# Normalising attention weights on VectorE before the transposes, in a four-layer Trainium2 kernel

## The chip, the cores and the metric

The kernel runs on one NeuronCore of one Trainium2 chip, as one program. The time is the device time of one execution in microseconds (us), the median of three runs. Engines: TensorE (PE, its weight loads are PEld), VectorE (DVE), ScalarE (ACT), GpSimd (POOL), and the DMA queues, most of them issued from SyncE (SP).

## What is computed

Sixteen sequences of 128 tokens with 512 features go through four residual updates: gated cross attention with 16 heads of 32 over a 128-token context, a ternary feed-forward layer, an attention over features, and a mixture of 16 experts. The change lies in the first, which the kernel interleaves with the second:

```python
q = (x @ wq.T).reshape(B, L, NH, HD)
k = (memory_tokens @ wk.T).reshape(B, M, NH, HD)
v = (memory_tokens @ wv.T).reshape(B, M, NH, HD)
attn = jnp.einsum('blhd,bmhd->bhlm', q, k) * scale
attn = jnp.where(memory_mask[:, None, None, :], attn, -jnp.inf)
attn = jax.nn.softmax(attn, axis=-1)
out = jnp.einsum('bhlm,bmhd->blhd', attn, v).reshape(B, L, C)
out = out @ wo.T
gate = jax.nn.sigmoid(x @ wg.T)
return gate * out
```

The ternary layer normalises each row of x, rounds it to 8 bits, and multiplies by weights of -1, 0 and 1. All projections of the attention are computed in three matmuls each (high by high, high by low, low by high part of each operand), so every operand is split by ScalarE (high part) and VectorE (the rest).

## The kernel before

`attention_heads_and_ternary` holds the first two layers. One list of steps, `plan`, is written out by hand as text, once for a group of four batches (GB = 4) and four times over (NG = 4, groups 0 to 3). Every engine walks the same list in the same order and does its own part of each step, so a step's place in the text is its place in the queue of every engine that has work in it. An engine stands still at a wait, and everything behind it in its queue stands still too. A number after a step is a batch, a half batch or a quarter batch (a unit of four heads), counted in the group; negative numbers are batches of the group before. `during` adds steps that only group 0 has: statistics of x (`sx`), scales (`xa`, `xb`, `xd`) and the ternary weights (`fq`, `ft`, `fg`).

The steps that matter here, with their work:

- `xT.b`, `cT.b`: four transposes on PE into a bank T, a ScalarE copy (high part), a VectorE subtraction (low part, L701).
- `q.p.j`, `k.p.j`: 12 matmuls on PE into a bank M, then a ScalarE copy (L591). `g.b`, `v.b`, `oP.b`: 12 wider matmuls into a bank M, emptied by ScalarE (`g`, L585) or VectorE (`v` L730, `oP` L737). `fm`: four bf16 matmuls, emptied by VectorE (L744).
- `Sa.t`, `Sb.t`: the score matmuls of a half batch. The step between the two, always a transpose, gives the first half time to drain. They fill both score banks SC.
- `sm.u`: for a unit of four heads VectorE takes the maxima (L753) and subtracts them (L758) into `pr`, ScalarE takes four exponentials in place and lets their sums accumulate (L597).
- `pT.u`: four transposes of `pr` into T, a ScalarE copy into `pT` (L569). `pv.t`: 8 products of attention weights and values, issued as 16 matmuls, into `O` (L530).
- `rc.b`: VectorE takes the reciprocals of the 16 sums of a batch (L763). `bc.b`: PE spreads them over a bank `REC`, in the layout of `O`, by 16 products with the identity, issued as 32 matmuls (L539); ScalarE copies the bank to `o` (L602). `on.b`: VectorE multiplies `O` by `o` (L767). `oT.b`: ScalarE rounds `o` to the high part (L606), VectorE subtracts (L771). `oP.b` multiplies by Wo.
- `u.b`: the quantising of a batch, six VectorE instructions that wait for each other (L652 to L659); `uT.b` transposes it. `ra`, `rb`, `rd`: row scales, seven, three and one small VectorE instruction with a GpSimd power between them. `st`, `sf`, `sx`: row statistics (L708). `nm`: normalised x. `mk`: mask rows.
- GpSimd adds `upd` to X after every `oP` and `fm` (L386, L394) and a bias in `uT` (L390). SyncE loads the next pair of contexts at each odd `cT` and the next masks at each fourth `mk`.

There are two banks T, two M, two SC, one O and one REC, eight in all. A step of kind T or M takes the bank of the step but one before it in the order of T or M steps, and waits until that one has been emptied, for `xT` and `cT` by both ScalarE and VectorE:

```python
tf = at(T_KINDS, s)
wait(pe, t_hi, tf - 2)
wait(pe, t_lo, up_to(T_KINDS, SPLIT, tf - 2))
```

Of the kernel before, what the change touches and what calls it, by code (L numbers as in the profile page):

```python
# [140 lines left out]
def attention_heads_and_ternary(nc, c, x, g_x, g_f, fw, fb, ctx_in, mask, norm_w, wq, wk, wv, wo, wg):  # L141

    X, identF = c["X"], c["identF"]
    with ExitStack() as st:
# [159 lines left out]
        with nc.Block() as block:  # L304
# [92 lines left out]
            def _(pe):  # L397
# [55 lines left out]
                for s in plan:  # L453
# [3 lines left out]
                    elif kind in T_KINDS:  # L457
# [63 lines left out]
                    elif kind == "pv":  # L521
                        b, half = t // 2, t % 2
                        pe.wait_ge(t_hi, at(T_KINDS, ("pT", 2 * t + 1)))
                        if half == 0:
# [7 lines left out]
                        i.then_inc(pv, 1)
                    elif kind == "bc":
                        pe.wait_ge(o_norm, 2 * t + 1)
                        wait(pe, r_out, t)
                        for j in range(KC):
                            for r in range(HQ):
                                at_ = col_of(j, r)
                                i = pe.matmul(REC[r * HD:(r + 1) * HD, j * S:(j + 1) * S],  # L539
                                              rec[:, t % 2, at_:at_ + 1].to_broadcast([P, HD]), identF[:, :],  # L540
                                              start=True, stop=True)
# [1311 lines left out]
```

## Time and profile before

| | us |
|---|---|
| median of 3 runs | 1397.67 |
| lowest and highest run | 1394.35 and 1404.95 |
| time of the profiled execution | 1401.04 |
| its span in the profile | 1399.3 |
| group 0 of the heads, from its first `Sa` to the next group's | 107.80 |
| group 1 | 103.25 |
| group 2 | 101.81 |
| group 3, first half and second half | 45.58 and 50.32 |

The profile is one execution. The profiled execution's own time lies 1.7 us above its span, and 3.4 us above the median of the runs. The four groups take from 40.4 to 449.2 us of the span. After them follow the last steps of the ternary layer, the attention over features, and the experts, which take more than half of the span.

### The profile page before, as it was taken

What the parts mean: (1) busy time and instruction counts of PE and PEld (TensorE: products, weight loads), DVE (VectorE), ACT (ScalarE), POOL (GpSimd) and SP (SyncE); (2) the same over time, 40 slices, a digit from 0 to 9 for tenths busy, and PEclk for the clock granted to TensorE, in tenths of its full rate; (3) what the DMA queues carried; (4) which work ended last, traced back from release to release, by engine and by line L of the source; (5) the groups of instructions that cost most, each with busy time, mean ns of one, the idle gap of its engine ahead of it and who ended that gap; (6) DMA issues with size and microseconds to landing.
All of it is one profiled execution on the core that took longest, in us unless ns stands there. A gap on an engine that the chain in (4) does not pass through costs nothing. (4 is left out here: it accounts for less than half of the span.)

```text
span 1399.3 us, 25475 instructions
## 1 busy us (share of the span) xinstructions
PE 1238.7 (89%) x7821; PEld 1041.0 (74%) x7822; DVE 719.3 (51%) x1443; ACT 553.9 (40%) x1430; POOL 426.3 (30%) x504
## 2 busy tenths in 40 slices
PE   6998999999996599789987896799999989999992
PEld 6876777777774377556766675689999878999992
DVE  5666655655655599854667532433234543434330
ACT  4543444444542388632111011433334543434340
POOL 1101211211212556520035601134444433344442
PEclk9999999999998699889999998899999999999996
DMA  9000000000000111322000202455446655545456
GB/s 319 24 22 12 17 1 18 17 1 17 1 2 1 46 42 41 115 88 73 1 0 1 92 30 77 143 140 137 76 80 139 182 124 143 137 82 131 88 137 165
DMA packets 53881, 103.62 MB, mean 74 GB/s; under 512 B 5127, under 2 KB 20999, under 8 KB 53751
## 3 DMA queue, kind: packets, MB, share of 16 engines
q1 hardware_dynamic: 38182, 65.78, 14.2%
q0 software_dynamic: 15632, 36.97, 13.9%
q8 instruction: 40, 0.66, 0.2%
q14 instruction: 27, 0.21, 0.0%
HBM read 75.99 MB, written 30.93 MB: 76 GB/s over the span
## 5 line engine op out<-in xcount | busy, mean ns | idle before, releaser
L1703 PE MATMUL t_H<-m_W,t_xT 128*128 128x352 f32 x1632 | 286.6, 332 | 15.8 <-DVE m_W L1781 14.1
L1703 PEld LDWEIGHTS t_H<-m_W,t_xT 128*128 128x128 f32 x1632 | 268.2, 193 | 18.1 <-DVE m_W L1781 14.6
L1670 POOL DMA_INDIRECT acc_d<-t_ys,t_sid x68 | 109.4, 1609 | 284.6 <-ACT t_ys L1732 200.7
L1748 ACT ACTIVATE t_sl<-t_H 128x352 f32<-128x352 f32 x68 | 31.5, 464 | 174.6 <-PE t_H L1703 174.6
L597 ACT ACTIVATE pr<-pr 128x128 f32<-128x128 f32 x256 | 76.1, 299 | 55.3 <-DVE pr L758 53.9
L62 PE MATMUL t_Y<-m_W,t_hT 128*128 128x512 f32 (+1 forms) x207 | 88.6, 428 | 9.9 <-DVE t_hT L1826 6.8
L1802 DVE TENSOR_TENSOR t_h<-t_H,t_sl 128x352 f32<-128x352 f32 x68 | 35.6, 523 | 106.3 <-ACT t_sl L1748 105.7
L1732 ACT ACTIVATE t_ys<-t_Y,t_wcol 128x512 f32<-128x512 f32 x69 | 47.4, 687 | 95.5 <-PE t_Y L64 88.1
L1824 DVE TENSOR_TENSOR t_hT<-t_TH,t_hT 128x256 fp32r<-128x256 f32 x68 | 28.8, 423 | 106.5 <-ACT t_hT L1769 105.3
L64 PE MATMUL t_Y<-m_W,t_hT 128*128 128x512 f32 (+1 forms) x207 | 82.6, 399 | 0.0
L63 PE MATMUL t_Y<-m_W,t_hT 128*128 128x512 f32 (+1 forms) x207 | 82.3, 398 | 0.0
L1644 POOL DMA_INDIRECT t_xg<-rows_d,t_gid x72 | 71.2, 990 | 22.1 <-issue 21.8
L386 POOL TENSOR_TENSOR X<-X,upd 128x512 f32<-128x512 f32 x16 | 20.4, 1273 | 157.0 <-DVE upd L737 157.0
L1161 POOL TENSOR_SCALAR m_W<-m_W,bst 128x128 fp32r<-128x128 f32 x64 | 55.7, 889 | 29.7 <-PE eL L1225 29.6
L373 POOL TENSOR_TENSOR tmp<-tmp,nhalf 128x2 f32<-128x2 f32 (+2 forms) x22 | 18.6, 848 | 144.9 <-DVE tmp L627 121.1
L753 DVE TENSOR_REDUCE mx<-SC 128x4 f32<-128x512 f32 x64 | 43.7, 684 | 32.7 <-PE SC L517 32.6
L569 ACT ACTIVATE pT<-T 128x512 f32<-128x512 f32 x64 | 38.0, 595 | 54.4 <-PE T L423 54.2
L1556 DVE SCALAR_TENSOR_TENSOR X<-eY,tg,X 128x512 f32<-128x512 f32 x32 | 23.9, 751 | 63.5 <-PE eY L64 63.4
L1280 ACT ACTIVATE ehT<-eh 128x512 fp32r<-128x512 f32 (+1 forms) x24 | 15.2, 633 | 99.8 <-DVE eh L1498 99.8
L1777 DVE TENSOR_TENSOR t_xT<-t_TX,t_xT 128x512 fp32r<-128x512 f32 x69 | 47.6, 690 | 12.1 <-issue 7.3
L62 PEld LDWEIGHTS t_Y<-m_W,t_hT 128*128 128x128 f32 (+1 forms) x207 | 39.6, 191 | 16.9 <-DVE m_W L1818 7.5
L1725 ACT ACTIVATE t_xT<-t_TX 128x512 fp32r<-128x512 f32 x69 | 41.4, 599 | 24.5 <-PE t_TX L1682 24.5
...
## 6 DMA issues: line engine op xcount, KB each, us to landing
...
m_r<-in_L_ffn_w_dram SPq DMA_DIRECT2D x13, 512.0 KB, 6.8
...
CT<-in_ctx_dram SPq DMA_DIRECT2D x8, 512.0 KB, 3.7
...
```

Source lines behind the costliest of these rows:

```text
L62: pe.matmul(out, lhs(0), rhs(0), start=first, stop=False)
L63: pe.matmul(out, lhs(0), rhs(1), start=False, stop=False)
L64: return pe.matmul(out, lhs(1), rhs(0), start=False, stop=last)
L597: i = act.activation(pp, pp, ACT.Exp, scale=SCALE0, accum_out=sums[:, t // HQ % 2, at_:at_ + 1])
L753: dve.tensor_reduce(mx[:, t % 2, :], bk, AX.X, ALU.max).then_inc(s_out, 1)
L1161: i = pool.tensor_scalar(tab_a[t % SLOTS][:, k, :], iP.bitcast(F32), place_p[:, t, k:k + 1], None, ALU.is_equal)
L1644: pool.indirect_dma_start(out=xg[:, b, :], out_offset=None, in_=m["rows_d"][:, :], in_offset=bass.IndirectOffsetOnAxis(ap=gid[:, b:b + 1], ...
L1670: pool.indirect_dma_start(out=m["acc_d"][:, :], out_offset=bass.IndirectOffsetOnAxis(ap=sid[:, b:b + 1], axis=0), in_=ys[:, b, :], in_offs ...
L1703: x_ = pe.matmul(bk[b % 2][:, 0:I], xT[:, b % 2, jx, k, :], W13[:, jw, k, j, :], start=k == 0 and jx == jw, stop=k == KC - 1 and jx == 1)
L1725: act.activation(xT[:, b % 2, 0, :, :], TX[:, :].rearrange("p (k t) -> p k t", k=KC), ACT.Copy).then_inc(tx_hi, 1)
L1732: act.activation(ys[:, (b - 1) % UT, :], Y[(b - 1) % 2][:, :], ACT.Copy, scale=wcol[:, (b - 1) % UT:(b - 1) % UT + 1]).then_inc(y_evac, 1)
L1777: dve.tensor_tensor(xT[:, b % 2, 1, :, :], TX[:, :].rearrange("p (k t) -> p k t", k=KC), xT[:, b % 2, 0, :, :].bitcast(F32), ALU.subtract) ...
```

## The change

The attention weights are divided by their sums before they are transposed. A new step `nr.u`, one for each unit of four heads (16 in a group), has VectorE take the four reciprocals of the unit and, after a wait for them, multiply the 128x512 tile `pr` in place by the reciprocals, broadcast along the keys. `pT.u` waits for this (`p_norm`) instead of the exponentials. `rc`, `bc` and `on` are gone, with the tile `o` and the bank REC. O gets that bank as its second one, alternating by batch, and `oT` reads O directly, on ScalarE and VectorE. `pv` of a batch waits for the `oT` of the batch two before. The text of the plan is written anew: `oP.2` and `g.3` move, most odd `pT` stay between `Sa` and `Sb`, most even ones move to just before `Sa`, `cT.3` moves ahead of `pT.0`, `fq.1` behind `v.1`.

```diff
         for g in range(NG):
             d = during.get(g, ("",) * 10)
             plan += steps(
-                f"Sa.0 xT.2 Sb.0 sm.0 sm.1 v.0 st.-2 st.-1 cT.2 ra.-1 xT.3 {d[0]} g.0 rb.-1 pT.0 cT.3 q.1.0 rd.-1 Sa.1 pT.1 Sb.1 "
-                f"sm.2 sm.3 mk.4 q.1.1 u.-2 {d[1]} pv.0 q.1.2 sf.-4 sf.-3 pT.2 uT.-2 u.-1 {d[2]} q.1.3 Sa.2 pT.3 rc.0 Sb.2 sm.4 sm.5 "
-                f"fm.-2 bc.0 pv.1 on.0 oT.0 k.1.0 uT.-1 {d[3]} k.1.1 pT.4 {d[4]} v.1 fm.-1 Sa.3 pT.5 Sb.3 sm.6 sm.7 mk.5 "
-                f"k.1.2 nm.4 nm.5 pv.2 k.1.3 pT.6 sf.-2 {d[5]} g.1 oP.0 Sa.4 pT.7 rc.1 Sb.4 sm.8 sm.9 "
-                f"xT.4 sf.-1 v.2 bc.1 pv.3 on.1 oT.1 pT.8 {d[6]} cT.4 g.2 xT.5 Sa.5 pT.9 Sb.5 sm.10 sm.11 mk.6 "
-                f"oP.1 cT.5 st.0 pv.4 q.2.0 pT.10 {d[7]} q.2.1 Sa.6 pT.11 rc.2 Sb.6 sm.12 sm.13 "
-                f"q.2.2 nm.6 nm.7 bc.2 pv.5 on.2 oT.2 {d[8]} q.2.3 st.1 pT.12 v.3 {d[9]} ra.0 Sa.7 pT.13 Sb.7 sm.14 sm.15 mk.7 "
-                f"k.2.0 rb.0 pv.6 k.2.1 rd.0 u.0 pT.14 uT.0 u.1 g.3 pT.15 rc.3 oP.2 bc.3 pv.7 on.3 oT.3 fm.0 k.2.2 uT.1 k.2.3 fm.1 "
-                f"oP.3 ", g)
+                f"Sa.0 xT.2 Sb.0 sm.0 sm.1 v.0 st.-2 st.-1 nr.0 cT.2 nr.1 ra.-1 xT.3 {d[0]} g.0 rb.-1 cT.3 pT.0 rd.-1 "
+                f"Sa.1 pT.1 Sb.1 sm.2 sm.3 mk.4 q.1.0 sf.-4 sf.-3 q.1.1 nr.2 u.-2 {d[1]} nr.3 q.1.2 pv.0 uT.-2 u.-1 {d[2]} q.1.3 pT.2 "
+                f"Sa.2 pT.3 Sb.2 sm.4 sm.5 fm.-2 oT.0 k.1.0 nr.4 uT.-1 {d[3]} pv.1 k.1.1 nr.5 v.1 {d[4]} fm.-1 pT.4 "
+                f"Sa.3 pT.5 Sb.3 sm.6 sm.7 mk.5 k.1.2 nm.4 nr.6 nm.5 pv.2 k.1.3 nr.7 sf.-2 {d[5]} g.1 oP.0 pT.6 "
+                f"Sa.4 pT.7 Sb.4 sm.8 sm.9 xT.4 sf.-1 v.2 nr.8 oT.1 pv.3 nr.9 {d[6]} cT.4 g.2 xT.5 pT.8 "
+                f"Sa.5 pT.9 Sb.5 sm.10 sm.11 mk.6 oP.1 cT.5 nr.10 st.0 pv.4 q.2.0 nr.11 {d[7]} q.2.1 pT.10 "
+                f"Sa.6 pT.11 Sb.6 sm.12 sm.13 q.2.2 nm.6 nr.12 nm.7 pv.5 q.2.3 oT.2 nr.13 {d[8]} st.1 g.3 v.3 {d[9]} ra.0 pT.12 "
+                f"Sa.7 pT.13 Sb.7 sm.14 sm.15 mk.7 k.2.0 rb.0 pv.6 k.2.1 nr.14 rd.0 u.0 oP.2 nr.15 uT.0 u.1 k.2.2 pT.14 fm.0 uT.1 "
+                f"pT.15 k.2.3 pv.7 fm.1 oT.3 oP.3 ", g)
...
@@ tensor
                         elif kind == "pT":
-                            pe.wait_ge(p_exp, t + 1)
+                            pe.wait_ge(p_norm, t + 1)
...
                         if half == 0:
                             pe.wait_ge(m_dve, at(BY_DVE, ("v", b)))
-                            wait(pe, o_norm, 2 * b)
+                            wait(pe, o_lo, b - 1)
...
@@ scalar
-                            pp, at_ = pr[:, t % 2, slot, :], t % HQ * HQ + slot
-                            i = act.activation(pp, pp, ACT.Exp, scale=SCALE0, accum_out=sums[:, t // HQ % 2, at_:at_ + 1])
+                            pp = pr[:, t % 2, slot, :]
+                            i = act.activation(pp, pp, ACT.Exp, scale=SCALE0, accum_out=sums[:, t % 2, slot:slot + 1])
...
                     elif kind == "oT":
-                        act.wait_ge(o_norm, 2 * t + 2)
+                        act.wait_ge(pv, 2 * t + 2)
                         wait(act, m_fill, at(M_KINDS, ("oP", t - 1)))
-                        act.activation(oT[:, 0, :, :].rearrange("p k t -> p (k t)"), o[:, :], ACT.Copy).then_inc(o_hi, 1)
+                        act.activation(oT[:, 0, :, :].rearrange("p k t -> p (k t)"), O[t % 2][:, :], ACT.Copy).then_inc(o_hi, 1)
...
@@ vector
+                    elif kind == "nr":
+                        dve.wait_ge(p_exp, t + 1)
+                        pp = pr[:, t % 2, :, :]
+                        dve.reciprocal(rec[:, t % 2, :], sums[:, t % 2, :]).then_inc(inverse, 1)
+                        dve.wait_ge(inverse, t + 1)
+                        dve.tensor_tensor(pp, pp, rec[:, t % 2, :].unsqueeze(2).to_broadcast([P, HQ, S]), ALU.mult)\
+                            .then_inc(p_norm, 1)
```

## Rows read from the trace of the kernel before

**Rows 1.** The page, part 1: engine, busy us, share, instructions.
```profile
PE 1238.7 (89%) x7821; PEld 1041.0 (74%) x7822; DVE 719.3 (51%) x1443; ACT 553.9 (40%) x1430; POOL 426.3 (30%) x504
```

**Rows 2.** Windows, groups 0, 1, 3: PE, PEld, DVE, ACT, POOL busy, clock, DMA.
```profile
40.44:148.24 107.80, 98.14 (x872) 80.85 (x873) 69.61 (x160) 49.55 (x190) 17.21 (x14) 0.98 0.06 19
148.24:251.49 103.25, 98.33 (x865) 79.92 (x865) 59.66 (x126) 47.55 (x184) 18.05 (x16) 0.98 0.04 12
353.30:398.88 45.58, 43.91 (x369) 35.51 (x369) 26.91 (x56) 21.95 (x89) 7.76 (x7) 1.00 0.00 1
398.88:449.20 50.32, 42.20 (x385) 31.84 (x384) 27.61 (x58) 21.06 (x83) 9.24 (x9) 0.90 0.01 1
```

**Rows 3.** Timeline: start us, duration us, engine, line, operation; from 241.5 us.
```profile
241.53 1.08 PE L539 MATMUL REC<-identF,rec 128*32 128x128 f32 x32
242.43 0.62 PE L530 MATMUL O<-pT,va 128*32 128x128 f32 x16
```

**Rows 4.** VectorE by line, 148 to 252 us: count, busy, mean ns, idle before.
```profile
L771 DVE TENSOR_TENSOR oT<-o,oT 128x512 fp32r<-128x512 f32 x4 | 2.8, 693 | 2.8 <-ACT oT L606 2.8
L767 DVE TENSOR_TENSOR o<-O,o 128x512 f32<-128x512 f32 x4 | 2.8, 690 | 3.6 <-ACT o L602 3.6
L763 DVE RECIPROCAL rec<-sums 128x16 f32<-128x16 f32 x4 | 1.0, 244 | 0.0
```

**Rows 5.** Timeline of VectorE, 162 and 166 us.
```profile
162.03 0.69 DVE L753 TENSOR_REDUCE mx<-SC 128x4 f32<-128x512 f32 x1 [2.01 <-PE SC L517]
162.76 0.69 DVE L758 TENSOR_TENSOR pr<-SC,mx 128x512 f32<-128x512 f32 x1
163.36 0.68 DVE L753 TENSOR_REDUCE mx<-SC 128x4 f32<-128x512 f32 x1
...
166.49 0.16 DVE L658 RECIPROCAL fsc<-fsc 128x1 f32<-128x1 f32 x1
166.69 0.48 DVE L659 TENSOR_SCALAR fu<-fu,fsc 128x512 f32<-128x512 f32 x1
```

**Rows 6.** Timeline, how a transpose waits for its bank, 156.8 us.
```profile
156.80 0.60 PE L423 MATMUL T<-identF,pr 128*128 128x128 f32 x4
157.10 0.69 DVE L701 TENSOR_TENSOR xT<-T,xT 128x512 fp32r<-128x512 f32 x1
157.89 0.63 PE L423 MATMUL T<-identF,CT 128*128 128x128 f32 x4 [0.50 <-issue]
```

**Rows 7.** Timeline, how a projection waits for ScalarE, 182.9 us.
```profile
182.93 0.71 PE L517 MATMUL SC<-kT,qT 32*128 32x128 f32 x8
...
185.20 0.64 PE L530 MATMUL O<-pT,va 128*32 128x128 f32 x16
...
188.06 0.19 PEld L62 LDWEIGHTS M<-Wg,xT 128*128 128x128 f32 x1 [0.38 <-ACT kT L591]
...
190.94 0.40 PE L62 MATMUL M<-Wo,oT 128*128 128x512 f32 x1
```

**Rows 8.** Timeline, a transpose waiting for VectorE at 233.6 us.
```profile
233.59 1.08 PE L423 MATMUL T<-identF,fu 128*128 128x128 f32 x4 [2.78 <-DVE fu L659]
```

**Rows 9.** Window behind that wait: busy by engine, then granted clock.
```profile
234.00:236.00 2.00, 2.00 (x8) 1.71 (x7) 1.23 (x2) 0.60 (x1) 0.00 (x0) 0.50 0.00 0
```

**Rows 10.** Timeline of group 0, a reduction that starts late.
```profile
108.19 0.71 PE L517 MATMUL SC<-kT,qT 32*128 32x128 f32 x8
...
111.87 0.63 DVE L753 TENSOR_REDUCE mx<-SC 128x4 f32<-128x512 f32 x1
```

**Rows 11.** L845 beside busy GpSimd: duration ns min/median/max; one slow instance.
```profile
L845 DVE TENSOR_TENSOR as<-asg,as x66: 673/678/1068, 480.8 to 580.1; 128x512 fp32r<-128x512 f32 x66
...
483.44 1.07 DVE L845 TENSOR_TENSOR as<-asg,as 128x512 fp32r<-128x512 f32 x1 [0.67 <-ACT as L901]
...
484.14 1.51 POOL L875 TENSOR_TENSOR ak<-aCX,ak 128x512 fp32r<-128x512 f32 x1 [0.18 <-POOL ak L873]
```

**Rows 12.** The page, part 6: a context load, KB and us to landing.
```profile
CT<-in_ctx_dram SPq DMA_DIRECT2D x8, 512.0 KB, 3.7
```

More of the change, by code:

```diff
@@ L170, in attention_heads_and_ternary @@
         mx = sb("mx", [P, 2, HQ])
-        sums, rec = sb("sums", [P, 2, NH]), sb("rec", [P, 2, NH])
-        o = sb("o", [P, D])
+        sums, rec = sb("sums", [P, 2, HQ]), sb("rec", [P, 2, HQ])
         oT = sb("oT", [P, 2, KC, S], F32R)
@@ L185, in attention_heads_and_ternary @@
         T, M, SC = bank("T", 2), bank("M", 2), bank("SC", 2)
-        O, REC = bank("O", 1)[0], bank("REC", 1)[0]
+        O = bank("O", 2)
         mask_f = dg[0:NB, :]
@@ L201, in attention_heads_and_ternary @@
         NU, NH2 = NB * HQ, 2 * NB
-        TILED = ("xT", "cT", "v", "g", "rc", "bc", "on", "oT", "oP", "st", "sf", "sx", "nm", "mk", "u", "uT", "fm")
+        TILED = ("xT", "cT", "v", "g", "oT", "oP", "st", "sf", "sx", "nm", "mk", "u", "uT", "fm")
         def steps(text, g):
@@ L221, in steps @@
                         continue
-                elif kind in ("sm", "pT"):
+                elif kind in ("sm", "nr", "pT"):
                     nums[0] += NQ * g
@@ L259, in attention_heads_and_ternary @@
         M_KINDS, X_UPD, STATS = BY_ACT + BY_DVE, ("oP", "fm"), ("sx", "st", "sf")
-        PV = ("pv", "bc")
         order = {}
@@ L264, in attention_heads_and_ternary @@
             order[kinds] = {s: i + 1 for i, s in enumerate([s for s in plan if s[0] in kinds])}
-        for kinds in (SPLIT, T_KINDS, BY_ACT, BY_DVE, M_KINDS, X_UPD, STATS, PV):
+        for kinds in (SPLIT, T_KINDS, BY_ACT, BY_DVE, M_KINDS, X_UPD, STATS):
             order[kinds] = {s: i + 1 for i, s in enumerate([s for s in plan if s[0] in kinds])}
@@ L290, in attention_heads_and_ternary @@
         s_half, s_fill, s_out, p_exp, pv = (sem(n) for n in ("s_half", "s_fill", "s_out", "p_exp", "pv"))
-        o_norm, r_out, o_hi, o_lo = (sem(n) for n in ("o_norm", "r_out", "o_hi", "o_lo"))
+        inverse, p_norm, o_hi, o_lo = (sem(n) for n in ("inverse", "p_norm", "o_hi", "o_lo"))
         added, biased, q_step, f_step = (sem(n) for n in ("added", "biased", "q_step", "f_step"))
         U_STEPS, F_STEPS = 6, 8
-        RING = SC + [O, REC]
-        def col_of(j, r):
-            return (j // 2 * 2 + r % 2) * HQ + r // 2 * 2 + j % 2
+        RING = SC + O
         def ctx_after(eng, s):
@@ L529, in _ @@
                             for r in range(HQ):
-                                i = pe.matmul(O[r * HD:(r + 1) * HD, j * S:(j + 1) * S], va[:, j * HQ + r, :],
+                                i = pe.matmul(O[b % 2][r * HD:(r + 1) * HD, j * S:(j + 1) * S], va[:, j * HQ + r, :],
                                               pT[:, r % 2, r // 2 * 2 + jj, :], start=True, stop=True)
[L532 to L541, printed above, removed]
                         i.then_inc(pv, 1)
@@ L567, in _ @@
                         elif kind == "pT":
-                            wait(act, pv, at(PV, ("pv", t // 2 - 1)))
+                            wait(act, pv, at(("pv",), ("pv", t // 2 - 1)))
                             act.activation(pT[:, t % 2, :, :].rearrange("p j m -> p (j m)"), src, ACT.Copy).then_inc(t_hi, 1)
@@ L728, in _ @@
                         dve.wait_ge(m_fill, mf)
-                        wait(dve, pv, at(PV, ("pv", 2 * t - 1)))
+                        wait(dve, pv, at(("pv",), ("pv", 2 * t - 1)))
                         dve.tensor_scalar(va[:, :, :], M[(mf - 1) % 2][:, :].rearrange("p (h d) -> p h d", h=NH),
@@ L759, in _ @@
                                           ALU.subtract).then_inc(s_out, 1)
-                    elif kind == "rc":
-                        dve.wait_ge(p_exp, HQ * t + HQ)
-                        wait(dve, pv, at(PV, ("bc", t - 2)))
-                        dve.reciprocal(rec[:, t % 2, :], sums[:, t % 2, :]).then_inc(o_norm, 1)
-                    elif kind == "on":
-                        dve.wait_ge(pv, at(PV, ("pv", 2 * t + 1)))
-                        dve.wait_ge(r_out, t + 1)
-                        dve.tensor_tensor(o[:, :], O[:, :], o[:, :], ALU.mult).then_inc(o_norm, 1)
+                    elif kind == "nr":
[5 more added lines that the diff above has]
+                            .then_inc(p_norm, 1)
                     elif kind == "oT":
@@ L770, in _ @@
                         dve.wait_ge(o_hi, t + 1)
-                        dve.tensor_tensor(lo_, o[:, :], hi_.bitcast(F32), ALU.subtract).then_inc(o_lo, 1)
+                        dve.tensor_tensor(lo_, O[t % 2][:, :], hi_.bitcast(F32), ALU.subtract).then_inc(o_lo, 1)
 def attention_features(nc, c, ctx_in):
```

4 lines of the change are left out of this document (removed).

## The prediction

> **What bounds the kernel now.** I read the page first: PE is busy 89% of the span [rows 1]. Then the windows of the four groups, which hold all that the change touches: they take 408.8 us, PE is busy in 98.33 of group 1's 103.25 us and VectorE in 59.66 [rows 2]. So PE sets the pace there, and what leaves PE's queue is time won, unless PE then waits for another engine. Last I read the timeline of group 1 for the places where PE does wait. They are of three kinds.
>
> A transpose waits until its bank T is emptied. cT.3 could follow pT.0 at 157.3 but starts at 157.89, right behind VectorE's subtraction for xT.3, which ran from 157.10 to 157.79 [rows 6].
>
> A projection waits until its bank M is emptied. Behind Sb.3 (182.93) PE has k.1.2, pv.2, k.1.3 and pT.6, and then g.1 waits for a ScalarE copy until 188.06, because that copy is queued behind the eight exponentials [rows 7]. So the first copy behind a pair of sm is through 5.1 us after Sb starts.
>
> A transpose waits for the quantising: uT.0 stands 2.78 us, for VectorE [rows 8], and in the 2 us behind it the granted clock is 0.50, the lower of the two levels (1.2 GHz) [rows 9].
>
> Summed over group 1, step by step, by which a step's length is the distance to the next start less its length elsewhere, PE loses about 8.5 us in this way: 3.0 at uT.0 and 1.0 in the slow clock behind it, 1.4 at uT.-2, 0.7 at cT.3, and eight losses of 0.2 to 0.6. That is more than the 4.9 us that the window shows as not busy, since a last matmul's modelled end covers part of a wait.
>
> **What goes.** bc occupies PE from 241.53 to the next start at 242.43, 0.90 us [rows 3], 16 times: 14.4 us, 3.6 in a group. On VectorE rc (0.24) and on (0.69) go, four of each in a group [rows 4], 3.7 us busy; the copy of REC leaves ScalarE.
>
> **What comes.** No nr is in the trace. Its multiply is a 128x512 tensor-tensor with both inputs in SBUF, as L771 is: 0.69 us [rows 4]. In the queue such an instruction takes 0.60 (162.76 to 163.36), and a reciprocal with a wait behind it 0.20 [rows 5]. So nr takes 0.81 us of the queue, 16 times: 13 us in a group. VectorE's load in group 1 rises from 59.7 to about 70 of 103 us: it stays below PE on average, but each nr pushes back everything behind it, and that has a price where PE waits for it.
>
> **Where PE waits in the new order.** I laid the new text against the durations of the trace, group 1, with time from Sa.0. A step v, g or oP takes PE 2.9 us and q or k 1.6 behind Sb (182.93 + 0.65 to 185.20), 1.5 elsewhere [rows 7], S with its transpose 2.0, a transpose 0.4, pv 0.6.
> - pT.0 now takes the bank of xT.3. Before, the subtraction for xT.3 started 8.86 us after Sa.0 [rows 2, 6]; now nr.0 and nr.1 stand ahead of it, and it ends at 8.86 + 1.62 + 0.69 = 11.2. PE is there at 9.2: 2.0 us. cT.3 and pT.1 lose 0.3 each in the same way.
> - q.1.2 needs the copy of q.1.0, which is behind the exponentials of sm.3, 5.1 us after Sb.1's start [rows 7]. PE has only 0.65 + 1.6 + 1.5 until then: 1.4 us. uT.-2 then waits 0.7 for u.-2, k.1.1 0.3.
> - g.1, g.3 and oP.2 come behind a projection, pv and a projection: 0.65 + 1.6 + 0.6 + 1.5 against 5.1, 0.8 us or, with the engine's reaction, 0.9 each.
> - pT.8 takes the bank of cT.4. From Sb.4's start the exponentials end at 4.7 and ScalarE copies xT.4 until 5.3; behind it VectorE has xT.4 0.6, sf 0.6, v 0.7, nr.8 0.8, oT.1 0.6, nr.9 0.8, cT.4 0.7: 10.1. PE has Sb, xT.4, v, pv, cT.4, g, xT.5: 8.1. It loses 2.0 us, where before it lost almost none.
> - At the end of the group, oP.2 (2.9) now stands ahead of uT.0, and covers u.0: the wait of 2.78 is gone. But uT.1 waits 1.1 (oP.2's drain, nr.15 and u.1 follow each other), and oP.3 waits 1.6, as VectorE has fm.1 and oT.3 to do after fm.1 has left PE.
>
> These come to 12.5 us. Group 1: -3.6 - 8.5 + 12.5 = **+0.4 us**; group 2 the same. Group 0 has `during` as well. Already before, its reduction behind Sb.6 starts 3.7 us after Sb's start (108.19, 111.87) where 0.75 is usual, as fq.3 and four sx are in front [rows 10]; now nr.10 and nr.11 are too, and fg.3 waits 5.2 us for the copy of q.2.2. With 1.8 at pT.1, 1.4 each at q.1.2, v.1 and fg.1, 3.4 at pT.8 and the end of the group as above its waits come to about 18 us, against about 13 read before (among them 3.0 at uT.0 and 3.5 behind the late reduction); less 3.6 for bc, it ends **1.7 us** later. In group 3 xT, cT, q.2 and k.2 are absent, and its second half has PE busy only 42.2 of 50.3 us [rows 2]: PE waits on chains. There the order pays: oP.2 fills the time of u.0, g.3 that of the exponentials. The first half ends 2.2 later, as in group 1. The second goes Sa.4 to Sa.5 in 8.7 us, to Sa.6 in 6.9, to Sa.7 in 9.1 (g.3 among them), and to the end of oP.3 in 20.5: 45.2 against 50.3, and a further 1.1 because the last update no longer waits for GpSimd: 2.2 - 5.1 - 1.1 = **-4.0 us**.
>
> The steps moved past SyncE's queue are cT.3 (a step earlier) and mk; a context lands in 3.7 us [rows 12] and is used a group later, so that costs nothing. The second O bank lets pv start without `on`; PE never waited there. Nothing behind the heads changes.
>
> **GpSimd beside nr.** The trace shows that a tensor-tensor with both inputs in SBUF can be slowed: L845 takes 0.67 to 0.68 us, but 1.07 at 483.44, while GpSimd runs [rows 11]. In the new order nr.15 stands right behind oP.2's update, which sets off GpSimd's add. I take 0.4 us once a group, on the way to uT.1: **+1.6**. The lowest bound is nothing, the highest 0.4 on every nr.
> The Trainium skill ("SBUF — State Buffer", "Who interferes with whom") says that a VectorE instruction with two SBUF inputs contends with a GpSimd instruction that reads SBUF, and that the loser waits out the whole instruction. The rows agree that the two meet, but with 0.4 us, not the whole instruction. By the rule in full a meeting could cost as much as one whole GpSimd instruction, and the sum would be that of the slower rival below.
>
> **Sum.** 1.7 + 0.4 + 0.4 - 4.0 + 1.6 = +0.1 us on the profiled execution's 1401.04. The median is 3.4 us below that, 1397.67; so I predict **1398 us**, no change. The clock I take as even: the waits of 2.78 that brought 0.50 go, two of 2.0 and in group 0 one of 5 come; a 5 us wait may cost 1 to 2 us more.
>
> **The rivals.**
> - *PE keeps what it is given.* My replay may place too many waits, for it adds one late engine to another. If PE loses in the new order what it lost before, only bc counts: -14.4, 1383 us; if uT.0's 4 us go too in three groups, 1371. For it: VectorE idles 40% of the group. Against: the two subtractions at pT.0 and pT.8 are plainly behind two nr each. Chance 0.16.
> - *VectorE's lateness is the pace (slower).* Five places in a group hang on nr: pT.0 and pT.8 by two each, uT.1 by one. If nr takes c, PE loses 5 (c - 0.81) more in each. With the slow multiply throughout, c = 1.2, that is 2 us a group, 1406 us; it is slower by over 1% from c = 1.5 on: 1412. If each nr waited out a GpSimd instruction of 1.5 us [rows 11], c would be 2.3, 7.5 us a group, 1428. Against: GpSimd is busy 18 of 103 us [rows 2], so most nr meet nothing. Chance 0.13. It is the rule of the Trainium skill's page "SBUF — State Buffer" (section "Who interferes with whom") that would bring this case about.
> - *My case*, within 1%: 0.71, its own range 1388 to 1408.
>
> **How the numbers follow.** 1% is 14 us, about what a measurement of this kernel tells from no change. Faster 0.16, same 0.71, slower 0.13. A wrong reading by 2 us of each group's waits moves the time by 8; the range reaches to the edge of both rivals, 1384 to 1410.
>
> **What would show it right or wrong.** In the changed kernel: L539 gone, 64 multiplies of 0.69 us at the new line, some at 1.1 beside GpSimd; groups 1 and 2 from Sa.0 to Sa.0 in 102 to 106 us; PE standing about 2 us at pT.0 and pT.8, both released by a subtraction of L701's kind; 1.4 at q.1.2, released by ScalarE; no wait at uT.0; VectorE busy near 70 us in group 1. If the groups take 100 us or less, the replay had waits too many; if pT.8 stands 3 us or more, nr is dearer than I took it.

## The result, and the profile after

The changed kernel takes **1426.61 us** (median of 4 runs, 1425.43 to 1427.83) against 1398.74 us before on the same chip: ratio **1.0183**, 95% interval 1.0155 to 1.0211. It is 28 us slower; the prediction was 1398 us, no change. The profiled execution took 1425.57 us, its span is 1423.9.

First the page, part 1 (compare [rows 1]): PE has 512 matmul records fewer and is busy 2.6 us longer. VectorE has 46 us more.

```profile
PE 1241.3 (87%) x7309; PEld 1038.1 (73%) x7310; DVE 765.5 (54%) x1539; ACT 547.1 (38%) x1414; POOL 426.0 (30%) x504
```

The windows of the changed kernel's four groups (compare [rows 2]; the number behind the busy times is the granted clock, then DMA share and GB/s):

```profile
40.76:160.26 119.50, 103.59 (x744) 83.48 (x744) 80.14 (x184) 47.85 (x186) 17.58 (x14) 0.90 0.06 17
160.26:270.88 110.62, 100.06 (x739) 80.81 (x739) 70.96 (x150) 46.08 (x180) 18.42 (x16) 0.94 0.04 11
270.88:376.90 106.02, 94.02 (x737) 75.49 (x737) 70.94 (x150) 45.76 (x180) 18.43 (x16) 1.00 0.03 11
376.90:479.75 102.85, 89.98 (x625) 68.38 (x624) 67.31 (x138) 41.24 (x168) 18.36 (x16) 0.88 0.00 1
```

Groups 2 and 3 of the kernel before, over the same steps:

```profile
251.49:353.39 101.90, 96.99 (x866) 78.82 (x866) 59.66 (x126) 47.53 (x184) 18.05 (x16) 1.00 0.04 12
353.39:449.39 96.00, 86.21 (x753) 67.35 (x752) 54.52 (x114) 43.01 (x172) 17.19 (x16) 0.95 0.01 1
```

The four groups of these two layers, from here on called the heads, take 438.99 us instead of 408.95: **+30.0**. Groups 1 and 2 run the same plan, and VectorE, ScalarE and GpSimd are busy equally long in both; yet group 1 is 4.6 us longer and PE is *busy* 6 us longer in it, at a clock of 0.94 against 1.00. What lies outside the heads is 5.4 us shorter than before. The change doesn't touch it; behind the heads the profiled executions of kernels with the same text differ by as much (944.2 us here, 949.9 before, 946.0 and 949.8 in later ones). So below I read a cause from the heads, and the median only for the total. Each kernel has one profile, and so one reading of its heads.

The multiply of nr, and the first instruction of a quantising, by duration in ns (minimum/median/maximum), then first and last start:

```profile
L744 DVE TENSOR_TENSOR pr<-pr,rec x64: 691/692/1789, 47.0 to 463.1; 128x512 f32<-128x512 f32 x64
...
L631 DVE TENSOR_SCALAR fu<-X,mean,rstd x16: 540/546/1486, 141.2 to 490.0; 128x512 f32<-128x512 f32 x16
```

Of the 64 multiplies 56 take the 0.69 us that I took from [rows 4]. Three take 1.17 or 1.18, and five 1.76 to 1.79: one at the end of each group and one in the middle of group 3. Even L631, which the change didn't touch, goes up to 1.49.

Then the waits of PE in the changed kernel, 40 to 480 us (us in total, times, longest):

```profile
PE T L416 <- DVE fu L638: 15.7, 8, 3.2
PE T L416 <- issue: 12.4, 8, 1.8
PE M L62 <- DVE oT L749: 6.1, 4, 1.5
PE M L62 <- ACT kT L574: 4.9, 7, 1.1
PE M L430 <- ACT qT L574: 4.3, 1, 4.3
PE M L62 <- ACT qT L574: 2.6, 3, 1.4
PE T L416 <- DVE pr L744: 2.2, 1, 2.2
```

The waits are where the replay had put them: "issue" is pT.0 and pT.8 at the bank (up to 1.8), then oP.3 (1.5), g.1, g.3 and oP.2, fg.3 in group 0 (4.3, `M L430`) and q.1.2. One line is too large: eight waits for `fu` come to 15.7 us. Three of them are uT.1 in groups 0 to 2, 2.85 us each, where I had 1.1; in group 3 uT.0 and uT.1 wait 3.17 and 2.14. The timeline at the end of group 2 shows why uT.1 waits so long:

```profile
363.03 0.17 DVE L742 RECIPROCAL rec<-sums 128x4 f32<-128x4 f32 x1
363.19 1.27 POOL L379 TENSOR_TENSOR X<-X,upd 128x512 f32<-128x512 f32 x1 [4.12 <-DVE upd L716]
363.23 1.78 DVE L744 TENSOR_TENSOR pr<-pr,rec 128x512 f32<-128x512 f32 x1
...
364.42 1.71 POOL L383 TENSOR_TENSOR X<-X,fbrow 128x512 f32<-128x512 f32 x1
364.94 1.48 DVE L631 TENSOR_SCALAR fu<-X,mean,rstd 128x512 f32<-128x512 f32 x1
...
368.38 0.63 PE L416 MATMUL T<-identF,fu 128*128 128x128 f32 x4 [2.85 <-DVE fu L638]
```

GpSimd's addition for oP.2 starts 0.04 us ahead of nr.15's multiply, which takes 1.09 us more than alone. GpSimd goes straight on to the bias addition of uT.0; the first instruction of u.1 takes 1.48 instead of 0.54. Together 2.03 us on the chain to uT.1, whose transpose waits 2.85.

And the clock, in windows of the changed kernel behind such waits (groups 0 and 3):

```profile
105.50:108.50 3.00, 3.00 (x9) 2.42 (x8) 2.80 (x5) 1.43 (x9) 0.00 (x0) 0.50 0.00 0
...
125.70:128.70 3.00, 2.97 (x8) 2.49 (x9) 2.22 (x8) 1.47 (x4) 0.17 (x1) 0.50 0.00 0
...
444.50:449.00 4.50, 4.50 (x31) 3.35 (x31) 3.40 (x6) 2.45 (x14) 0.00 (x0) 0.54 0.00 0
```

0.50 is the lower level, 1.2 GHz. The first stretch follows a wait of 1.7 us at pT.8, the second one of 4.3 at fg.3, the third one of 2.2 at pT.10. PE is busy throughout, but slowly: three matmuls of a wide projection take 1.28 us from start to start there, and 0.70 elsewhere.

Such a wait is not always followed by a slow stretch. Groups 1 and 2 have the same waits at pT.0, pT.8, uT.1 and oP.3. Here is pT.0 in each:

```profile
171.46 0.63 PE L416 MATMUL T<-identF,pr 128*128 128x128 f32 x4 [1.78 <-issue]
282.07 0.63 PE L416 MATMUL T<-identF,pr 128*128 128x128 f32 x4 [1.79 <-issue]
```

Behind the first the clock falls to 0.50 until 179; behind the second, and in the whole of group 2, it stays at 1.00. What decides between the two the runs don't show.

**Theory.** Most of the 28 us is two prices that I set too low: TensorE's slow clock behind waits of 2 to 3 us, and GpSimd holding up VectorE once in a group. **Rivals.** The multiplies as such load VectorE too much; or the order of the steps is at fault, whichever mechanism it carries.

### The profile page after: what moved, and what is told of

Read it like the earlier page. It is cut to its first block and busy times, and to the rows that moved or that the text cites. A ratio compares the mean times of both kernels' runs of the same rounds, so it can differ in the third digit from the quotient of the medians.

```text
span 1423.9 us, 24472 instructions
## 1 busy us (share of the span) xinstructions
PE 1241.3 (87%) x7309; PEld 1038.1 (73%) x7310; DVE 765.5 (54%) x1539; ACT 547.1 (38%) x1414; POOL 426.0 (30%) x504
## 5 line engine op out<-in xcount | busy, mean ns | idle before, releaser
L1681 PE MATMUL t_H<-m_W,t_xT 128*128 128x352 f32 x1632 | 285.6, 331 | 15.4 <-DVE m_W L1759 13.9
L1681 PEld LDWEIGHTS t_H<-m_W,t_xT 128*128 128x128 f32 x1632 | 267.2, 192 | 17.8 <-DVE m_W L1759 14.4
L416 PE MATMUL T<-identF,pr 128*128 128x128 f32 x256 | 42.7, 292 | 14.6 <-issue 12.4
L744 DVE TENSOR_TENSOR pr<-pr,rec 128x512 f32<-128x512 f32 x64 | 51.2, 800 | 2.2
```

Of the source, the lines that this page charges most:

```text
L744: dve.tensor_tensor(pp, pp, rec[:, t % 2, :].unsqueeze(2).to_broadcast([P, HQ, S]), ALU.mult)\
L1681: x_ = pe.matmul(bk[b % 2][:, 0:I], xT[:, b % 2, jx, k, :], W13[:, jw, k, j, :], start=k == 0 and jx == jw, stop=k == KC - 1 and jx == 1)
```

## Experiments

Times are medians; the kernel before ran beside them at 1398.4 to 1399.6 us.

### e1: GpSimd's additions later

```diff
 # GpSimd, oP
                         pool.wait_ge(m_dve, at(BY_DVE, s))
+                        if t % GB == 2:
+                            pool.wait_ge(q_step, U_STEPS * (t - 1) + 1)
 # GpSimd, uT: uT.0's bias addition waits for all of u.1
-                        pool.wait_ge(q_step, U_STEPS * t + 1)
+                        pool.wait_ge(q_step, U_STEPS * (t + 2 if t % GB == 0 else t) + (0 if t % GB == 0 else 1))
```

> The changed kernel, but GpSimd holds back two adds of each group: that of oP.2 until u.1's first instruction is done, and the bias add of uT.0 until all of u.1 is done. In the changed kernel nr.15's multiply takes 1.78 us there instead of 0.69, and u.1's first instruction 1.48 instead of 0.54. Theory G (GpSimd beside VectorE's two-input multiply is what was mis-sized): both go back to 0.69 and 0.54, the wait at uT.1 falls from 2.85 to about 1 us, and four groups save 8 us, with some clock behind it up to 12: 1415 to 1419. Theory C (the clock behind long waits) alone: only what the shorter uT.1 wait saves in clock, 2 to 4 us: 1423. Theory O (the order as such): no change, 1426.

Measured: 1415.15 us, ratio 1.0112 (1.0085 to 1.0139), as the theory of the collision expected; heads 429.48, 9.5 shorter than the changed kernel's. The ten runs spread widely, from 1402.24 us at a mean clock of 0.948 to 1420.63 at 0.933, and the profile is of the slowest, so the 9.5 is a rough figure. In e1's timeline both instructions have their usual length again:

```profile
355.90 0.69 DVE L746 TENSOR_TENSOR pr<-pr,rec 128x512 f32<-128x512 f32 x1
356.51 0.54 DVE L633 TENSOR_SCALAR fu<-X,mean,rstd 128x512 f32<-128x512 f32 x1
357.08 0.69 DVE L636 TENSOR_REDUCE fsc<-fu 128x1 f32<-128x512 f32 x1
357.19 1.27 POOL L381 TENSOR_TENSOR X<-X,upd 128x512 f32<-128x512 f32 x1 [5.46 <-DVE fu L633]
```

The stretch from Sa.7 of group 2 to the next Sa.0 has the full clock in both kernels. It goes from 24.12 to 22.09 us: **2.03 us**, what the two instructions had too much in the changed kernel. The collision is shown, and its price. The last two rows also show why the addition costs nothing in its new place: beside it a reduction, with one input, takes 0.69 us, as it does alone.

### e2: filler transposes in PE's waits

```diff
+                def warm(n):
+                    b = (done_pv[0] + 1) // 2
+                    wait(pe, o_lo, b - 1)
+                    for i in range(n):
+                        pe.transpose(O[b % 2][:, i % KC * P:(i % KC + 1) * P], identF[:, :], identF[:, :])
+                WARM = {("pT", 0): 15, ("q", 1, 2): 8, ("g", 1): 3, ("pT", 8): 15, ("g", 3): 3, ("oP", 2): 4, ("uT", 1): 25,
+                        ("oP", 3): 14, ...}
 ...
                 for s in plan:
+                    if warm_of(s):
+                        warm(warm_of(s))
```

> The changed kernel, but ahead of the long waits of PE it issues transposes of the identity into the O bank that is free at that time, as many as fill the wait of the changed kernel to some tenths of a us (15 ahead of pT.0 and pT.8, 25 ahead of uT.1, 14 ahead of oP.3, 38 ahead of fg.3 in group 0). The waits themselves stay. Theory C: the granted clock stays at 1.0 in the groups, the steps behind the waits take 2.9 instead of 3.9 to 5.2 us, and the time falls by 10 to 15 us: 1411 to 1416. Theory G or O: the clock costs nothing on the path, 1426 or a little more for fillers that are too long.

Measured: 1411.13 us, ratio 1.0084 (1.006 to 1.0108). Windows of e2's groups:

```profile
40.05:152.13 112.08, 108.99 (x880) 90.73 (x881) 80.17 (x184) 47.69 (x186) 17.63 (x14) 1.00 0.07 18
152.13:258.23 106.10, 103.58 (x824) 85.01 (x824) 70.98 (x150) 45.84 (x180) 18.49 (x16) 1.00 0.04 12
258.23:364.30 106.07, 103.62 (x825) 85.02 (x825) 70.98 (x150) 45.84 (x180) 18.48 (x16) 1.00 0.04 11
364.30:462.44 98.14, 93.78 (x745) 75.15 (x744) 67.30 (x138) 41.05 (x168) 18.45 (x16) 1.00 0.00 1
```

PE has more to do and the heads are **16.6 us** shorter: 7.4, 4.5, 0.0 and 4.7 by group, just where the clock had been below 1.00. The median fell by 15.5, as the theory of the clock expected. The slow clock is shown, and its price in these executions.

### e3: the multiply left out

```diff
-                        dve.reciprocal(rec[:, t % 2, :], sums[:, t % 2, :]).then_inc(inverse, 1)
-                        dve.wait_ge(inverse, t + 1)
-                        dve.tensor_tensor(pp, pp, rec[:, t % 2, :].unsqueeze(2).to_broadcast([P, HQ, S]), ALU.mult)...
+                        dve.reciprocal(rec[:, t % 2, :], sums[:, t % 2, :]).then_inc(p_norm, 1)
```

> The changed kernel without nr's multiply: only the reciprocals are taken, and the attention weights are left undivided. VectorE has 64 instructions of 0.69 us and their 18 us of stretching less. The load theory (VectorE's added work is the loss, by whichever way): pT.0 and pT.8 wait 0.6 to 0.8 instead of 1.8, uT.1 none, at most 1398. Theory O (the new order costs by itself, at the M banks: q.1.2, g.1, g.3, oP.2): the waits at these stay, and the time stays above 1405.

The attention weights are not divided, so other tokens go to other experts and the median (1415.14) can't be read; the heads can. They take 402.65 us, with groups of 107.41, 100.44, 100.39 and 94.41, at clocks of 0.98, 1.00, 1.00 and 0.93. So with the multiply goes more than the whole loss, 36.3 us: it is the root, and the waits, the clock and the collision are the ways in which it costs. Beside e2 (group 2: 106.07) the multiply costs 5.7 us in a group at full clock. The stretch from Sa.7 has 2.0 of it, the collision; the rest lies in the stretches with pT.0 (1.5), from Sa.1 to Sa.2 (0.7) and with pT.8 (1.5). Without it the new order beats the group of before at full clock (101.90) by only 1.5 us of bc's 3.6. I put the rest down to the order's waits: in e3 the projections wait 11.7 us for ScalarE, 3.2 before, and oP.3 waits 1.5 us in each group. That is read from the lists of waits, not tested. Neither expectation asked for the heads; the waits at q.1.2 and its like stayed, as theory O had it.

### e4: nr in the order of before

```diff
-                f"Sa.0 xT.2 Sb.0 sm.0 sm.1 v.0 st.-2 st.-1 nr.0 cT.2 nr.1 ra.-1 xT.3 {d[0]} g.0 rb.-1 cT.3 pT.0 rd.-1 "
+                f"Sa.0 xT.2 Sb.0 sm.0 sm.1 v.0 st.-2 st.-1 nr.0 cT.2 nr.1 ra.-1 xT.3 {d[0]} g.0 rb.-1 pT.0 cT.3 q.1.0 rd.-1 Sa.1 pT.1 Sb.1 "
...
```

> VectorE scales as in the changed kernel, but PE's steps stand in the order of the kernel before (pT.8 ahead of cT.4, g.3 between uT.0 and pT.15, oP.2 behind pT.15, q.1.0 ahead of Sa.1), nr just ahead of where its pT needs it, nr.15 ahead of u.1 and so before oP.2's add. Theory O: without the new order the waits of PE stay at those of the kernel before plus the late subtractions, bc is saved, and the time is 1390 to 1400. The load theory: 64 nr cost wherever they stand, above 1415.

Measured: 1421.94 us, ratio 1.0165 (1.0128 to 1.0203); heads 434.78. The first waits of e4's list:

```profile
PE T L416 <- DVE pr L744: 18.7, 18, 3.5
PE T L416 <- DVE fu L638: 10.5, 6, 1.8
```

In the old order eighteen transposes wait for the multiply itself, so the even pT had a reason to move. But the new order as a whole is no better (438.99): its own waits are at the banks and the end of the group, and its clock is lower (0.90, 0.94, 1.00, 0.88 against e4's 0.94, 0.97, 0.97, 0.90). The time fits the expectation that nr costs wherever it stands; e8 below shows that it need not.

### e5: e1 and e2 together

The two edits above, with fewer fillers at uT.1 (8).

> The changed kernel with both edits at once: GpSimd's two adds held back as in e1_late_add, and the fillers of e2_fill (8 instead of 25 ahead of uT.1, since the wait there is shorter now). Two causes that add up: e2_fill's heads took 422.4 us; each group loses the 2.0 us of meeting with GpSimd at uT.1: 414 us for the heads and about 1403 in all. If GpSimd mattered in e1_late_add only through the clock (its shorter wait keeps TensorE fast, which the fillers do as well), then nothing is left to gain: 1411.

Measured: 1401.20 us, ratio 1.0017 (0.9997 to 1.0037), heads 414.13. Windows of its groups 1 and 3:

```profile
149.68:253.68 104.00, 101.63 (x807) 83.16 (x807) 68.93 (x150) 45.78 (x180) 18.07 (x16) 1.00 0.04 12
...
357.70:453.79 96.09, 92.62 (x734) 73.97 (x733) 65.25 (x138) 41.01 (x168) 18.03 (x16) 1.00 0.00 1
```

With both causes gone the time of before is back, as the first expectation had it, and group 1 takes the 103.65 us of the replay within 0.35. From e2 to e5 the heads lose 8.3 us, 2.07 a group. The two causes take 24.9 of the 30.0 us in the heads; alone they took 9.5 (e1) and 16.6 (e2), so they hardly overlap. Fillers aren't free where PE didn't wait: in group 3 nothing holds pT.8, and its 15 fillers make the stretch from Sa.4 to Sa.5 10.61 us long, 8.99 in the changed kernel.

### e6: the new order with the bank REC

```diff
 # before.py: rc, bc, on, the tile o and REC stay; the text of the plan is the changed one
+                f"Sa.2 pT.3 rc.0 Sb.2 sm.4 sm.5 fm.-2 k.1.0 uT.-1 {d[3]} bc.0 pv.1 on.0 oT.0 k.1.1 v.1 {d[4]} fm.-1 pT.4 "
...
```

> The kernel before (reciprocals spread by PE over REC, no nr) in the new order of steps, with rc, bc and on put beside pv and oT. The order alone. If the new order as such is no loss, and it was nr on VectorE that made the waits: the heads take 395 to 410 us and the time is 1385 to 1400 (oP.2 covers u.0, no nr ahead of the subtractions). If the order itself costs at the M banks (q.1.2, g.1, g.3, oP.2 behind the exponentials), the heads take over 415 us and the time is above 1405.

Measured: 1410.65 us, ratio 1.0075 (1.0051 to 1.0099), heads 424.38. So the order alone costs 15.4 us, nr alone 25.8 (e4), both together 30.0. The rival that blames the order is right for its part: without any nr PE waits 1.4 us at q.1.2 in each group, and the clock is 0.97, 0.98, 0.97 and 0.93. How much of the 15.4 is clock is not shown, for no fillers were run in this order. A part of e6's loss is of its own kind: REC's chain rc, bc, on, oT is late at the end of the group, and oP.3 waits 2.9 us for it, four times (1.5 in the changed kernel).

### e7: fillers in the kernel before

The same fillers, written into the bank REC, at uT.0 (25), uT.2 (9) and in the last group.

> The kernel before with fillers (transposes of the identity into the free bank REC): 25 ahead of uT.0 and 9 ahead of uT.2 of each group, 12 and 25 ahead of pT.12 and pT.14 in group 3. Theory C says that the clock costs before too, though less: the heads of before have a granted clock of 0.98, 0.98, 1.00 and 0.95 by group. If all of that comes back: 2 + 1 + 0 + 4 us, 1391 to 1394. If the clock was no cost before: 1398.

Measured: 1396.68 us, ratio 0.9983 (0.9963 to 1.0003), heads 409.24. Window of group 1:

```profile
147.81:249.69 101.88, 100.69 (x900) 82.54 (x901) 59.66 (x126) 47.49 (x184) 18.05 (x16) 1.00 0.04 12
```

The heads are no shorter than before (408.95): the fillers win 1.4 us in group 1, and group 3 is 1.7 us longer with them (97.73), though its clock rises from 0.95 to 0.98. So fillers bring the kernel before nothing in sum; what the clock alone costs in its group 3 is not separated from what the fillers there cost.

### e8: nr spread out, with an order of its own

```diff
+                f"Sa.0 xT.2 Sb.0 sm.0 sm.1 v.0 nr.0 st.-2 st.-1 cT.2 xT.3 g.0 nr.1 ra.-1 {d[0]} pT.0 cT.3 rb.-1 q.1.0 rd.-1 "
+                f"Sa.1 pT.1 Sb.1 sm.2 sm.3 mk.4 q.1.1 u.-2 {d[1]} pv.0 nr.2 q.1.2 nr.3 q.1.3 uT.-2 pT.2 u.-1 {d[2]} "
+                f"Sa.2 pT.3 Sb.2 sm.4 sm.5 fm.-2 nr.4 pv.1 oT.0 k.1.0 uT.-1 {d[3]} k.1.1 nr.5 sf.-4 sf.-3 pT.4 {d[4]} v.1 fm.-1 "
+                f"Sa.3 pT.5 Sb.3 sm.6 sm.7 mk.5 nr.6 k.1.2 nm.4 nm.5 pv.2 nr.7 k.1.3 pT.6 sf.-2 {d[5]} g.1 oP.0 "
+                f"Sa.4 pT.7 Sb.4 sm.8 sm.9 nr.8 xT.4 v.2 pv.3 oT.1 sf.-1 pT.8 nr.9 {d[6]} g.2 cT.4 xT.5 "
+                f"Sa.5 pT.9 Sb.5 sm.10 sm.11 mk.6 nr.10 oP.1 cT.5 st.0 pv.4 q.2.0 nr.11 {d[7]} q.2.1 pT.10 "
+                f"Sa.6 pT.11 Sb.6 sm.12 sm.13 nr.12 q.2.2 nm.6 nm.7 nr.13 pv.5 q.2.3 pT.12 oT.2 {d[8]} st.1 g.3 v.3 {d[9]} ra.0 "
+                f"Sa.7 pT.13 Sb.7 sm.14 sm.15 mk.7 nr.14 k.2.0 rb.0 pv.6 k.2.1 rd.0 pT.14 u.0 nr.15 oP.2 uT.0 u.1 k.2.2 pT.15 "
+                f"pv.7 oT.3 uT.1 fm.0 k.2.3 fm.1 oP.3 ", g)
 # and e1's edit; in group 0 sx.8 to sx.15 stand two to three chunks earlier; no fillers
```

> The changed kernel's nr with an order of steps of my own, laid out by the waits found: nr.0 ahead of the statistics and cT.2, nr.1 behind xT.3, pT.0 ahead of cT.3 again, q.1.0 ahead of Sa.1, pT.6, pT.8, pT.12 and pT.14 right behind a pair of projections, cT.4 behind g.2, nr.10 ahead of oP.1's update and nr.15 ahead of oP.2's, oT.3 ahead of uT.1, the statistics of group 0 spread over more steps; GpSimd's adds held back as in e1_late_add. If VectorE's load as such (71 us of a group) is the limit, the groups stay at 102 us or more. If only the places of nr were wrong, a group takes 95 to 98 us, the heads 385 to 395, and the time is 1370 to 1385, below both kernels.

Measured: **1375.06 us**, ratio **0.9815** (0.9781 to 0.9849), heads 390.80. Windows of e8's groups:

```profile
41.15:140.86 99.71, 93.59 (x745) 76.09 (x747) 78.04 (x184) 47.12 (x186) 17.75 (x14) 1.00 0.07 21
140.86:237.78 96.92, 94.39 (x738) 75.43 (x739) 69.75 (x150) 45.38 (x180) 18.48 (x16) 1.00 0.04 13
...
334.69:431.95 97.26, 85.87 (x625) 65.91 (x624) 65.97 (x138) 40.95 (x168) 18.41 (x16) 0.91 0.00 1
```

VectorE is busy 69.75 us in group 1, hardly less than in the changed kernel, and the group takes 96.92 instead of 110.62. The rival "VectorE is too full" has fallen: what counts is what stands behind each nr. The text puts at most one nr ahead of each piece of VectorE's work that PE needs next. In groups 1 and 2 no wait of PE is over 0.9 us, in group 0 two transposes wait for nr (1.3 and 1.1), and the clock stays at 1.00 in all three without fillers. VectorE still meets GpSimd, once in each of groups 1 to 3, with multiplies of 1.80 and 0.97 us one behind the other; nobody waits for them there. In group 3, where no xT, cT, q and k lie between, transposes wait for nr (1.1, 2.8 and 3.2 us); the first of these multiplies meets GpSimd too, and takes 1.18.

### e9: an order of its own for the last group

```diff
-                f"Sa.4 pT.7 Sb.4 sm.8 sm.9 nr.8 xT.4 v.2 pv.3 oT.1 sf.-1 pT.8 nr.9 {d[6]} g.2 cT.4 xT.5 "
+                f"Sa.4 pT.7 Sb.4 sm.8 sm.9 nr.8 v.2 pv.3 oT.1 sf.-1 g.2 nr.9 pT.8 "
...
-                f"Sa.7 pT.13 Sb.7 ... nr.14 k.2.0 rb.0 pv.6 k.2.1 rd.0 pT.14 u.0 nr.15 oP.2 uT.0 u.1 ...
+                f"Sa.7 pT.13 rd.0 Sb.7 sm.14 sm.15 nr.14 pv.6 u.0 nr.15 oP.2 pT.14 uT.0 u.1 pT.15 pv.7 oT.3 fm.0 uT.1 fm.1 oP.3 "
```

The steps ra.0, rb.0 and rd.0 come earlier in every group.

> e8's kernel with an order of its own for the last group, where e8 waited on VectorE's nr: pT.8, pT.12 and pT.14 stand one chunk later there (g.2, g.3 and oP.2 ahead of them), and ra.0 and rb.0 come earlier in every group. Theory (the cost of nr is only where it stands): group 3 goes from the 97.3 us of e8 to 89 to 92 us, the other groups stay at 96 to 97, the median is 1366 to 1371 us. Rival (the 64 multiplies keep the last group at VectorE's pace, wherever the transposes stand): group 3 stays at 96 to 98 us and the median at 1374 to 1378.

Measured: 1375.27 us, ratio 0.9843 (0.9811 to 0.9875); heads 387.80, group 3 94.86, the others 99.50, 96.72, 96.72. Group 3 lies between the two expectations, and the median has not moved, as the rival had it. Two windows of its group 3 show the rest:

```profile
392.00:402.00 10.00, 8.90 (x55) 6.55 (x54) 6.35 (x12) 3.75 (x18) 1.26 (x1) 0.66 0.00 0
...
417.00:427.18 10.18, 9.21 (x40) 5.38 (x40) 3.12 (x7) 1.22 (x3) 5.65 (x5) 0.60 0.00 0
```

Waits of 1.1 to 1.7 us remain at both, and the clock behind them is 0.66 and 0.60; if the work there ran at the full clock it would be some 3 and 4 us shorter, an estimate from the two windows, which would bring group 3 to 88. Fillers on top were not tried.

### e10: e8's order with the bank REC

```diff
 # rc, bc, on, the tile o and REC as before; e8's text without nr, e1's edit and sx as in e8
+                f"Sa.2 pT.3 rc.0 Sb.2 sm.4 sm.5 fm.-2 bc.0 pv.1 on.0 oT.0 k.1.0 uT.-1 {d[3]} k.1.1 sf.-4 sf.-3 pT.4 {d[4]} v.1 fm.-1 "
...
```

> The order of e8, the late additions of GpSimd and the places of sx, with the mechanism of before: rc, bc and on again, no nr, the bank REC, one bank O. It tells what the scaling ahead of the transposes is worth once the order is right. Theory A (the change's idea pays: bc costs TensorE 0.9 us sixteen times, and oT waits for on besides): 0.9 to 2 us more in each pair of chunks than e8, heads 14 to 30 us longer than e8's 390.8, median 1390 to 1405 us. Rival B (all of e8's gain is its order, the multiplies cost what bc did): heads 385 to 392, median 1370 to 1376.

Measured: 1380.70 us, ratio 0.9875 (0.9848 to 0.9902), heads 392.12. Windows of its groups 1 and 3:

```profile
140.15:239.54 99.39, 96.83 (x865) 78.97 (x865) 59.38 (x126) 47.40 (x184) 18.01 (x16) 1.00 0.04 13
...
338.95:431.65 92.70, 84.51 (x753) 66.52 (x752) 54.42 (x114) 42.97 (x172) 17.82 (x16) 0.98 0.00 1
```

Nearer to rival B. Of the 18.2 us by which e8's heads are shorter than before, **16.8 come from the order alone** (GpSimd's later additions among it). In the same order, scaling ahead of the transposes gives **1.3** more: 2.5 in each of groups 1 and 2, of bc's 3.6, and 0.9 in group 0; in group 3 it costs 4.6. With an order of its own for the last group (e9) the idea is 4.3 us ahead of e10, but bc was never given such an order. The medians lie further apart than the heads, 1375.06 against 1380.70; e8's profile is of its slowest run (1379.58) and e10's of its fastest (1377.72), so one profile each can't place the other 4 us.

### e11: e8 without the hold on GpSimd

```diff
-                        if t % GB == 2:
-                            pool.wait_ge(q_step, U_STEPS * (t - 1) + 1)
-                        pool.wait_ge(q_step, U_STEPS * (t + 2 if t % GB == 0 else t) + (0 if t % GB == 0 else 1))
+                        pool.wait_ge(q_step, U_STEPS * t + 1)
```

> e8 without the hold on GpSimd: the addition of oP.2 starts as soon as its input is there and the bias addition of uT.0 beside u.1. Theory (GpSimd beside VectorE's two-operand instructions costs 2.0 us a group where the quantising stands late in the group, as e1 against after): seg 7 from 20.2 to 21.5 to 22.3, the median 1380 to 1386 us. Rival (e1's gain came from the places of the steps around it alone, and in e8's order the collision lies behind other work of TensorE): 1374 to 1377 us.

Measured: 1384.05 us, ratio 0.9887 (0.9854 to 0.9919); heads 392.09, groups 100.41, 97.62, 97.64, 96.42. e8's order has nr.15 ahead of oP.2's update, so this multiply meets no addition. Another instruction does, the last one of u.1:

```profile
230.65 2.68 POOL L382 TENSOR_TENSOR X<-X,fbrow 128x512 f32<-128x512 f32 x2
230.69 0.16 DVE L636 RECIPROCAL fsc<-fsc 128x1 f32<-128x1 f32 x1
230.89 1.31 DVE L637 TENSOR_SCALAR fu<-fu,fsc 128x512 f32<-128x512 f32 x1
```

It takes 0.49 elsewhere: 0.8 too much, and the stretch from Sa.7 to the next Sa.0 (`seg 7` above) goes from 20.22 to 20.94, about half of the least that I expected. The median moved 9 us, which the heads (+1.3) don't explain; behind them this profile has 949.8 us against e8's 946.0. I take the collision as 0.7 us in each of groups 0 to 2, and leave the rest open.

## Why the prediction was wrong

**What held.** bc's 512 matmuls are gone, nr takes 0.17 and 0.69 us, VectorE is busy near 70 us in group 1 (70.96), and the waits stand at their places: pT.0 1.79 (2.0 predicted), pT.8 1.7 (2.0), q.1.2 1.4 (1.4), oP.3 1.53 (1.6), fg.3 4.3 (5.2), none at uT.0 in groups 0 to 2. In group 3 uT.0 did wait, 3.17 us. The wait at pT.0 in group 3, beside [rows 6]:

```profile
385.68 0.63 PE L416 MATMUL T<-identF,CT 128*128 128x128 f32 x4
388.10 0.63 PE L416 MATMUL T<-identF,pr 128*128 128x128 f32 x4 [1.79 <-issue]
```

**"The clock I take as even."** This step failed, and is the largest: 16.6 us (e2). I had weighed waits that go against waits that come by their length, 2.78 against 2.0, and put 1 to 2 us on the longest alone. But [rows 9] showed 0.50 behind one such wait, and my own list then had two waits of about 2 us and three of over 1 in each group, plus larger ones in group 0. Each was a chance, not a certainty, of a slow stretch, 3 to 10 us long in the changed kernel, in which all that PE does takes up to twice as long. The list called for a price on each, and a rival of its own.

**"I take 0.4 us once a group, on the way to uT.1: +1.6."** The place was right (nr.15 beside the addition that oP.2's update sets off); the size was five times too small. Measured: 1.09 on the multiply and 0.94 on u.1's first instruction, 2.07 a group, 8.3 us (e2 to e5). I had taken the one slow instance of [rows 11] and read it beside the wrong GpSimd instruction, the addition that starts 0.70 us after it. What runs when it starts is a shorter one:

```profile
483.35 0.61 POOL L873 CAST ak<-aCX 128x512 fp32r<-128x512 f32 x1 [2.15 <-PE aSC L64]
```

Of this 0.52 us was left, and the multiply lost 0.4; of the 1.27 us addition 1.23 was left, and nr.15 lost 1.09. I also counted one instruction, where GpSimd had two in a row. The Trainium skill ("SBUF — State Buffer", "Who interferes with whom") says that the loser waits out the whole instruction. Here the trace nearly agrees: 1.78 us is the addition's remaining 1.23 and then 0.55, where the multiply alone takes 0.69. In the slower rival this mechanism was right, but its price was put on every nr; 8 of the 64 meet GpSimd, and the five dear ones decide. That its dearest case, 1428 us, lies next to the measured 1426.6 is chance: more than half of the loss is the clock, which it did not have.

**Group 3, "-4.0".** Measured +6.85, of which 4.7 is clock and 2.0 the collision. In e5, without either, it took 96.09, 4.1 over the replay's 92.0. The first half came out as replayed (2.05 us later than before, against 2.2), and so did Sa.6 to Sa.7 (8.95 against 9.1) and from there to the end (20.60 against 20.5). The pieces Sa.4 to Sa.5 (10.6 against 8.7; 9.0 without fillers) and Sa.5 to Sa.6 (8.4 against 6.9) did not. The last term, -1.1 for the last update, does not show up in this window; no run separates it. The piece Sa.5 to Sa.6 holds a collision that I had not placed, here in the changed kernel:

```profile
439.27 1.26 POOL L379 TENSOR_TENSOR X<-X,upd 128x512 f32<-128x512 f32 x1 [13.15 <-DVE upd L716]
439.31 1.76 DVE L744 TENSOR_TENSOR pr<-pr,rec 128x512 f32<-128x512 f32 x1
...
441.22 0.63 PE L416 MATMUL T<-identF,pr 128*128 128x128 f32 x4 [2.18 <-DVE pr L744]
```

oP.1's update and nr.10 follow each other just as oP.2's and nr.15 do.

**"Group 2 the same."** Group 2 took 101.90 before, at the full clock, not 103.25. The replayed length of 103.65 is +1.75 against that, not +0.4.

**The sum again,** heads against before: 16.6 (clock, changed kernel to e2) + 8.3 (GpSimd, e2 to e5) + 5.2 (e5 to before, all the rest). These are the steps from one measured kernel to the next, so they make up the 30.0 by themselves; what they test is each term. I had 0, 1.6 and -1.5. By group the rest is 2.2, 0.8, 2.1 and 0.1 us, where the replay had 1.7, 0.4, 0.4 and -4.0.

**The faster rival.** "PE keeps what it is given" was wrong about this order. In another one the idea does come out ahead: e8 takes 1375 us, between that rival's 1371 and 1383. But nine tenths of its gain in the heads are due to the order and could be had with bc (e10), so that this rival's reason, bc's 14.4 us, is not what made e8 fast.
